# A two-layer graph network on one core: four input slots in the second edge loop, and a four-stage pipeline in the node passes

## What is computed

```python
# layer 0, x: [6250, 128]
scores = einsum('ehd,ehd->eh', q[dst], k[src]) / sqrt(16)
alpha  = softmax of scores over the edges of one dst
agg    = segment_sum(alpha * v[src], dst)
h1  = layer_norm(x + agg @ W0, ln1)
out = layer_norm(h1 + relu(h1 @ fc1 + b) @ fc2 + b, ln2)
x   = layernorm(x + out)
# layer 1, for each half (f: edges 0..49999, b: the rest)
h_e = relu(concat(x[src], edge_attr, req) @ W1 + b1) @ W2 + b2
h   = (1 + eps) * x + segment_sum(h_f, dst_f) + segment_sum(h_b, dst_b)
out = layernorm(x + relu(h @ Wu + bu))
```

## Time and profile before

| | |
|---|---|
| median of 3 runs | 2862.45 us (2857.86 to 2866.96) |
| profiled execution, its own time | 2882.01 us |
| its span, first to last instruction | 2880.1 us |
| first edge loop | until about 1355 us |
| node passes | about 1355 to 1601 us |
| second edge loop | about 1614 to 2880 us |
| busy: PE, VectorE, GpSimd, ScalarE | 55%, 50%, 54%, 26% |

### The profile page before, as it was taken

One profiled execution on the slowest core, in us unless ns is written; L12 is line 12 of the kernel. 1 busy time (PEld: TensorE's weight loads), 2 busy tenths in 40 slices (PEclk: granted clock), 3 DMA queues, 4 the chain that ended last, 5 costly groups with the idle time before them and its releaser, 6 DMA issues.

```text
span 2880.1 us, 32266 instructions
## 1 busy us (share of the span) xinstructions
PE 1588.5 (55%) x7344; PEld 1255.8 (44%) x7345; DVE 1430.9 (50%) x2992; ACT 746.1 (26%) x1502; POOL 1566.9 (54%) x1648
## 2 busy tenths in 40 slices
PE   5315556565556565555777345555555555555546
PEld 3215555555555555554555233333433333333424
DVE  3226666666666666666555234343443333344435
ACT  2213333333333333333454111111111111111111
POOL 3346666666666666663111455655666665556653
PEclk8557676767776777776998667766676666666667
DMA  5474444444444444441000112211221121112211
GB/s 167 138 200 127 143 131 141 131 138 133 129 142 131 141 131 138 133 128 60 18 27 27 56 42 51 52 49 48 54 51 51 50 52 50 47 48 51 53 49 38
DMA packets 148162, 255.22 MB, mean 89 GB/s; under 512 B 73948, under 2 KB 99088, under 8 KB 147996
## 3 DMA queue, kind: packets, MB, share of 16 engines
q0 software_dynamic: 65072, 160.39, 19.9%
q1 hardware_dynamic: 81186, 92.67, 10.1%
q10 hardware_dynamic: 1870, 1.78, 0.2%
HBM read 233.05 MB, written 28.04 MB: 91 GB/s over the span
## 4 chain that ended last, share of the span: by engine, by line
issue 33%; PE 22%; DVE 16%; another core or an unknown queue 13%; DVEq 5%; DMA 5%; ACT 4%; SPq 1%; POOL 0%; ACTq 0%; POOLq 0%
PE ps L1090 8%; PE ps L1050 6%; DVE arena L1566 3%; DVE arena L1435 2%; DVE arena L1575 2%; PE ps L1200 2%; DVEq L1595 2%; PE ps L1187 1%; ACT arena L873 1%; PE ps L1152 1%; DVEq L1594 1%; DVE arena L1440 1%; DMA first<-d 1%; DVEq L1592 1%
## 5 line engine op out<-in xcount | busy, mean ns | idle before, releaser
L710 POOL DMA_INDIRECT arena<-y_tab,arena x784 | 741.9, 946 | 512.6 <-issue 494.1
L657 POOL DMA_INDIRECT arena<-kvq_tab,arena x784 | 749.0, 955 | 471.3 <-issue 240.6
L1050 PE MATMUL ps<-arena 128*128 128x128 f32 x1596 | 325.7, 363 | 331.0 <-issue 251.4
L1200 PEld LDWEIGHTS ps<-arena 128*128 128x128 f32 x1568 | 285.5, 247 | 413.2 <-issue 394.1
L1200 PE MATMUL ps<-arena 128*128 128x128 f32 x1568 | 308.0, 336 | 282.8 <-issue 273.5
L1050 PEld LDWEIGHTS ps<-arena 128*128 128x128 f32 x1596 | 299.5, 275 | 349.9 <-issue 345.5
L1090 PE MATMUL ps<-arena 128*128 128x136 f32 x1568 | 319.2, 391 | 173.3 <-DVE arena L1440 88.5
L1090 PEld LDWEIGHTS ps<-arena 128*128 128x128 f32 x1568 | 309.5, 295 | 190.6 <-issue 190.6
L940 ACT ACTIVATE arena<-arena 128x512 f32<-128x512 f32 x224 | 118.9, 567 | 1029.7 <-DVE arena L1575 662.7
L1575 DVE TENSOR_TENSOR arena<-ps,arena 128x512 f32<-128x512 f32 x224 | 127.8, 616 | 511.2 <-remote 299.1
L1187 PE MATMUL ps<-w1blk,eaT 113*128 x456 | 271.3, 677 | 59.4 <-issue 55.6
(11 more groups left out here) (243 smaller groups left out, 1980.5 us busy)
## 6 DMA issues: line engine op xcount, KB each, us to landing
arena<-d SPq DMA_DIRECT2D x58, 897.0 KB
arena<-kvq_tab,arena POOLq DMA_INDIRECT x784
arena<-y_tab,arena POOLq DMA_INDIRECT x784
eat<-ea SPq DMA_DIRECT2D x59, 112.0 KB
ea<-in_edge_attr_dram SPq DMA_DIRECT2D x2, 3125.0 KB, 20.0
y_tab<-arena SPq DMA_DIRECT2D x10, 625.0 KB
kvq_tab<-arena SPq DMA_DIRECT2D x6, 937.5 KB
arena<-kvq_tab SPq DMA_DIRECT2D x59, 64.0 KB
```

The costliest lines, as they stand in the source:

```text
L657: g.indirect_dma_start(kv_s[:, r, t, :], None, kvq_tab.rearrange("n (a d) -> (n a) d", a=3), bass.IndirectOffsetOnAxis(ap=v3(idx, RING)[:, ...
L710: g.indirect_dma_start(yg_s[:, r, t, :], None, y_tab, bass.IndirectOffsetOnAxis(ap=v3(idx1, 2)[:, u, t:t + 1], axis=0)).then_inc(m_g[r][k] ...
L1050: last = mm(bank(k)[:, t * D:(t + 1) * D], hotT_s[:, u, s0 + t, :], v3(qwin, 2)[:, u, :])
L1200: last = mm(bank(6 + u)[:, 0:W], yg_s[:, r, t, :], hot1_s[:, u, t, :], start=(t == 0), stop=(t == G - 1))
```

## The change

1. `eat`, `idx1` and `dcol1` get four slots each; `eat` moves into the shared arena. The semaphores `m_ld`, `m_at`, `m_ix` become four each.
2. SP has one function `load_chunk`, which reads one offset and issues all three loads. In the loop it is called for chunk c+4 after one wait: that VectorE has read the last piece of chunk c. The waits for `m_eT` and `m_dcr` go.
3. The first four chunks are loaded before the node passes' stores begin.
4. POOL's waits at pieces 1 and 2 (`m_eTp`, `m_u`) go.
5. The node passes get a fourth stage `out_`: the product with layer 1's weights and its copy are done one pass later, at the head of the pass, while `old` is in its norms. The product moves to PSUM banks 1 to 3 (`rows_y`), `hidden` no longer waits for the copy, and the copy is two instructions. The transposition of `old` is placed between the third and the fourth of the five tiles of the second feed-forward product. ScalarE does the third norm of `old` before it takes the square root for `new`. The body of the loop runs seven times, with three passes before it and three after.
6. POOL's clearing of the accumulators moves from ahead of the passes to inside the first one. Waits at the end of POOL's and ACT's programs go, and SP waits for all loads at the end.

```diff
         def passes3(eng, one_pass):
-            one_pass(0, None, None)
-            one_pass(1, 0, None)
-            with eng.Fori(0, GROUPS - 2) as i:
-                one_pass(i + 2, i + 1, i)
-            one_pass(None, GROUPS - 1, GROUPS - 2)
-            one_pass(None, None, GROUPS - 1)
+            one_pass(0, None, None, None)
+            one_pass(1, 0, None, None)
+            one_pass(2, 1, 0, None)
+            with eng.Fori(0, GROUPS - 3) as i:
+                one_pass(i + 3, i + 2, i + 1, i)
+            one_pass(None, GROUPS - 1, GROUPS - 2, GROUPS - 3)
+            one_pass(None, None, GROUPS - 1, GROUPS - 2)
+            one_pass(None, None, None, GROUPS - 1)
...
+            sp.wait_ge(l_over, 4)
+            sp.wait_ge(s_eac, 32)
+            sp.wait_ge(s_tabi[1], 48)
+            def load_chunk(chunk, r):
+                off = sp.value_load(tab_sb[1][0:1, ds(5 * chunk, 1)], min_val=0, max_val=NB * CH)
+                sp.dma_start(eat_s[:, r, :], ea1[ds(off, CH), :].rearrange("(p g) f -> p (g f)", g=G)).then_inc(m_at[r], 16)
+                sp.dma_start(v3(idx1, RING)[:, r, :], i1[ds(off, CH)].rearrange("(p g) -> p g", g=G)).then_inc(m_ix[r], 16)
+                sp.dma_start(v3(dcol1, RING)[:, r, :], d1[ds(off, CH)].rearrange("(p g) -> p g", g=G)).then_inc(m_ld[r], 16)
+            for c in range(RING):
+                load_chunk(c, c)
...
             def sp_msgs(r, new, a_, b_, c_):
                 if new is not None:
-                    next_attr(new + 3, 1 - u)
                     sp.wait_ge(s_eac, 32)
                     sp.wait_ge(m_hid, spent)
-                    sp.wait_ge(m_dcr, prepared)
-                    load_edges(new + 2, u)
+                    load_chunk(new + RING, r)
...
             def gather_edges(r):
-                pool.wait_ge(m_ix[u], landed)
+                pool.wait_ge(m_ix[r], landed)
                 pool.wait_ge(m_agg, slot_free)
                 for k, (s0, n) in enumerate(PIECES):
-                    if k in (1, 2):
-                        pool.wait_ge(m_buf, 4)
-                        pool.wait_ge(*((m_eTp, turned_) if k == 1 else (m_u, asked)))
...
+            def pe_pass(new, mid, old, out_):
                 if mid is not None:
                     pe.wait_ge(n_h1, mid + 1)
                     transposes(h1, n_hTp)
+                if old is not None:
+                    pe.wait_ge(n_z, old + 1)
+                if out_ is not None:
+                    pe.wait_ge(n_xT, out_ + 1)
+                    for t in range(GRP):
+                        last = mm(rows_y(t), nTx[:, t * P:(t + 1) * P], w1x[:, :])
+                    last.then_inc(n_y, 1)
+                if mid is not None:
                     pe.wait_ge(n_hT, mid + 1)
-                    pe.wait_ge(n_ys, 1 if old is None else old + 1)
                     hidden(mid, 0)
                     hidden(mid, 1)
```

More of the change, by code:

```diff
@@ L535, in _ @@
             sp.wait_ge(f_dma, stored)
+            for r in range(RING):
+                sp.wait_ge(s_eac, 32)
+                sp.wait_ge(m_at[r], loaded)
+                sp.wait_ge(m_ix[r], loaded)
+                sp.wait_ge(m_ld[r], loaded)
         @block.gpsimd
@@ L607, in _ @@
             store_rows(6)
-            g.memset(eat[:, :], 0.0)
             g.memset(eaT[:, :], 1.0)
@@ L897, in act_pass @@
                 if new is not None:
+                    sqrt(0, new, norm1)
                     act.wait_ge(n_r[0], new + 1)
@@ L947, in act_msgs @@
                     act_relu(r, 1)
-                    if u:
+                    if r == RING - 1:
                         act.reg_add(landed_, landed_, 16)
-                    act_rows(new + 1, 1 - u, now)
+                    act_rows(new + 1, (r + 1) % RING, now)
                     act_relu(r, 2)
@@ L971, in _ @@
             passes4(act, act_msgs, n1)
-            act.wait_ge(m_buf, 4)
-            act.wait_ge(m_ld[1], landed_)
-            a.activation(mark[:, 2:3], eps_ln[:, :], ACT.Copy)
         @block.tensor
@@ L1134, in pe_pass @@
                 if mid is not None:
-                    pe.wait_ge(n_f1s, mid * FC + 2)
-                    hidden(mid, 3)
-                    pe.wait_ge(n_f1s, mid * FC + FC)
-                    if old is not None:
-                        pe.wait_ge(n_v[1], old + 1)
+                    for c in range(2, FC):
+                        pe.wait_ge(n_f1s, mid * FC + (c - 1))
+                        hidden(mid, c)
                     for t in range(GRP):
+                        if t == GRP - 2 and old is not None:
+                            turn_rows(new, old)
                         for c in range(FC):
+                            if t == 0:
+                                pe.wait_ge(n_f1s, mid * FC + (c + 1))
                             last = mm(bank(2, 2)[:, t * D:(t + 1) * D], v3(ffT, FC)[:, c, t * P:(t + 1) * P], fc2_sb[:, c, :],
@@ L1144, in pe_pass, with turn_rows @@
                     last.then_inc(n_f2, 1)
-                if old is not None:
-                    if new is not None:
-                        pe.wait_ge(n_v[0], new + 1)
-                    pe.wait_ge(n_x1, old + 1)
-                    transposes(res2, n_xTp)
-                    pe.wait_ge(n_xT, old + 1)
-                    for t in range(GRP):
-                        last = mm(bank(4, 3)[:, t * 2 * D:(t + 1) * 2 * D], nTx[:, t * P:(t + 1) * P], w1x[:, :])
-                    last.then_inc(n_y, 1)
+                elif old is not None:
+                    turn_rows(new, old)
+            def turn_rows(new, old):
+                if new is not None:
+                    pe.wait_ge(n_v[0], new + 1)
+                pe.wait_ge(n_x1, old + 1)
+                transposes(res2, n_xTp)
             pe.sem_inc(n_xTp, 1)
```

126 lines of the change are left out of this document (49 added, 77 removed).

## The result

| | before | after |
|---|---|---|
| median (4 runs each) | 2860.84 us | 2755.49 us (2752.38 to 2763.55) |
| ratio | | 0.9633, 95% interval 0.9607 to 0.966 |
| profiled execution's span | 2880.1 | 2755.1 |
| first loop, first to last gather | 1194.4 | 1178.3 |
| node passes, barrier to barrier | 252.3 | 204.8 |

The last row is counted from the start of the last gather. The forecast was 2826 us, range 2770 to 2885. The kernel is 105 us faster, nearly three times the forecast's 36.

What follows compares the result with a forecast made beforehand. A chain across engines bounds the node passes; POOL's gathers and pauses, with PE behind the longer ones, pace the second loop. Terms: 2882 - 31 - 5 = 2846; from the runs' median, 2862.45 - 36 = 2826 us, range 2770 to 2885.

Steps and rivals of the forecast that it cites:

- Node passes, -31 forecast: Node passes: a fourth stage takes product and copy off the pass's end; -31 us, bounds -37 and +28 for the seven intervals.
- the pass of 19.2 us: Node passes, steady body: each pass falls from 23.15 to 19.2 us, seven intervals saving 27.7 us.
- The chain without clock losses: Node passes: the new chain by PE and ACT from one h1 to the next, 17.9 us with handovers.
- the 1.3 us for low clock: Node passes: allowance per pass for PE's matmuls at a mean granted clock of 0.86, taking 17.9 to 19.2 us.
- filling and draining: Node passes, short passes around the steady body: one more to drain, others shed product and copy; together 3 us off.
- -40: Node passes: by the skill's clock rule, fewer gaps keep PE's clock at full level, giving -37 - 3 = -40 us.
- The entry, -5: Between node passes and second loop: early loads shrink the 6.8 us from barrier to first gather; -5 us, between 0 and -6.8.
- The second loop, 0 forecast: Second loop: PE needs pauses, so 5.0 us of pauses per chunk replace 4.6; taken as 0, bounds -98 and +106 us.
- That pause: Second loop: POOL, four chunks ahead, stands at `m_agg` for PE, about 10 us per two chunks, 5.0 per chunk.
- B: Rival, second loop: POOL streams up to four chunks while PE crawls, 1.9 us more per chunk; 2932 us, chance 0.10.
- A: Rival, second loop: PE's stalls shrink and the short pause goes, saving 98 us; 2728 us, chance 0.12.
- D: Rival, second loop: late instruction fetch makes the crawl, shorter SP code takes 25 us off the short pauses; 2801, chance 0.03.

Runs made afterwards that it cites:

- e7: Changed kernel with the first feed-forward product waiting for the copy again, and indices and columns loaded for chunk c+2 instead of c+4: 2839.3 us against 2863.1 before.
- e8: Changed kernel with the transposition behind the whole second feed-forward product; register additions on PE never reached the chip: 2761.2 us against 2863.1 before.
- e6: Changed kernel with the old order of square roots and norms, and POOL held by VectorE's last add of chunk c-2: 2784.8 us against 2863.1 before.
- e12: Changed kernel, three second-loop stretches: SP's offset read twice, 8 more PE matmuls per chunk, POOL waiting piece by piece: 2760.08 us against 2860.52 before.
- e13: Changed kernel with POOL's gathers waiting for PE's chunk c-3, then c-2, then c-4, in three stretches: 2789.54 us against 2891.98 before.
- e17: Changed kernel, POOL waiting only ahead of every second chunk (chunks 4 to 19), also inside each chunk (20 to 35), then unaltered: 2796.45 us against 2861.72 before.
- e18: Changed kernel with POOL's two waits inside a chunk put back, whole, on a chip with the stalls: 2762.6 us against 2889.45 before, ratio 0.957.
- e5_after: The changed kernel, unaltered, run again on a chip without the stalls: 2382.61 us against 2433.31 before, ratio 0.979.

## Why the prediction was wrong

- **Node passes, -31 forecast, -47.5 measured.** The mechanism was right, the size off. The term was the pass of 19.2 us: it is 17.2, which makes 14 of the missing 16.5 us. The chain without clock losses was 0.7 too long (17.9), and the 1.3 us for low clock didn't come. The rest, 2.5 us, is in filling and draining, where I had taken off 3. The Trainium skill, TensorE: Matmul & The Clock Gate (HAM oscillation), would have had -40 here by the forecast's own working; the trace agrees with its direction, since all products of the body run at 2.4 GHz (2.43 us), and e7 and e8 have slow ones again (4.11, and 3.35 to 4.47) where PE idles 1.6 and 1.1 us more in the pass. I took the clock as a property of the stage, while it moved with the gaps that the change closes.
- **The entry, -5:** -4.8.
- **The second loop, 0 forecast, -53 to -62 measured.** This is the step that failed: "That pause lasts some 5 us until PE is awake, and then until PE has finished the rest of its chunk, up to 7 us of work: about 10 us per two chunks". Such pauses exist, 6.7 us each, but they are 10 of 42. In the other 32 PE had no rest of the chunk to do: POOL waited only for the late update of `m_agg`, which in most of them came 2.5 to 2.9 us after the gathers stopped, and the pause took 3.3 to 3.7. I had missed that the first loop shows just such a pause of some 3.5 us in every chunk. They come up in the second loop once no longer wait covers them, and they are nearly enough for PE. So pauses of 4.65 us per chunk (260.8 / 56) became 3.3 (185.7 / 56), where the forecast had 5.0. Of the 80 us that the gathers gain, 18 go to a longer tail: PE is some three chunks behind when the last gather is out.
- **What the gain came from.** Per chunk, over chunks 4 to 51: changed kernel 20.8 us, held by VectorE's add of chunk c-2 21.6 (e6), by the load of indices behind it 22.3 (e7), before 22.2. The load and its 2.6 us are 0.7, VectorE as the gate the other 0.9. SP's shorter program (e12) and the depth by itself (e13) showed no gain, and neither did removing POOL's waits inside a chunk: with them the loop is no slower (e17, e18).
- **The rivals.** B, slower, was a real mechanism with the price I gave it (13 us per two chunks, e17), but it needs a stream of two chunks without a wait. A's short pause went, but shorter ones took its place, so some 53 to 62 of its 98 us came. D: the rule on instruction fetch (the Trainium skill, Runtime: NRT & Kernel Launch, Instruction fetch mechanics) isn't borne out; SP's longer program changed nothing (e12), and the instruction queues carried 12 and 23 packets, where they had 12 and 22.
- The range left out A's side; a term of "0" between -98 and +106 should have had most of its width.

## What to carry to other kernels

A long wait may be covering a shorter one: look in a neighbouring loop for what remains when the long one is gone. An instruction that has ended isn't yet a wait that is met: before a pause is called needless, compare it with the time at which its semaphore changed. Keep the producer of a ring off any chain of three hands (VectorE's add, SP's load, a DMA) and gate it by the engine that it may starve. With the stalls here, a few waits for work long done were cheap, and a long stream without one was dear (e17). Moving work into the gaps of the matmul engine can pay twice, as in the node passes, where its slow products went too.

## What the hardware showed

- The same program takes 2433 or 2861 or 2890 us, and the difference is whether PE's matmuls come 2 us apart, with `issue` as the reason, while POOL's gathers stream. On a chip without the stalls neither loop has one. Which condition decides stays open; one chip number showed both (runs e5_after and e18_meter_again).
- With the stalls, PE's updates of semaphores come late while POOL's gathers stream: in 32 of 42 pauses `m_agg` changes 4.5 us or more after the matmul that raises it, and mostly 2.5 to 2.9 us after the gathers stop. POOL and VectorE stand until then. Without the stalls the update follows its matmul within 0.02 us. What holds the updates back stays open, and so does whether it is the same thing that spaces out PE's matmuls. Why VectorE's add is dearer as a gate (e6) is shown only in part.
